# Cross attention and ternary feed-forward on one core: scores from two float32r row halves instead of six bfloat16 parts, and the copy of a group's sums on ScalarE

## The reference

```
q = rope(layernorm(x) @ Wq); k, v = split(ctx @ Wkv); k = rope(k)      # 32 heads of 16
w = softmax(q k^T / 4);  x = x + (w v) @ Wout + bout
u = absmax_quant(layernorm(layernorm(x)));  h = gelu(u @ ternary(w_fc)^T)
x = x + absmax_quant(layernorm(h)) @ ternary(w_proj)^T
```

## Time and profile before

| what | value |
|---|---|
| runs | 826.62, 828.09, 830.45 us |
| the profiled execution | 829.01 us; its span 826.9 us, 2.1 us lie around it |
| projection, to the first transposed score | 0 to 163 us |
| attention | 163 to 540 us |
| feed-forward | 540 to 827 us |
| TensorE / VectorE / ScalarE / GpSimd busy in the span | 782.2 / 683.7 / 454.8 / 337.3 us |

### The profile page before, as it was taken

The page is one execution under the profiler, slowest core; times in us unless marked ns, Lnnn a source line. Parts: engine busy times, 40 slices in busy tenths (PEclk is TensorE's granted clock), DMA queues, the critical chain, the costliest instruction groups (busy, mean ns, idle before and its releaser), DMA issues.

```text
span 826.9 us, 11697 instructions
## 1 busy us (share of the span) xinstructions
PE 782.2 (95%) x3842; PEld 333.4 (40%) x3842; DVE 683.7 (83%) x937; ACT 454.8 (55%) x825; POOL 337.3 (41%) x428
## 2 busy tenths in 40 slices
PE   1899999799999999999999999998999999999995
PEld 0788877122222222222232222243444444444442
DVE  5988876988888888888888887279999899899883
ACT  4477655177777777777777777642233322333230
POOL 3777866645434554455445554221113111111000
PEclk9999999599999999999999999999999999999998
DMA  8288886634555555665666663226565455643553
GB/s 280 83 213 237 251 232 169 160 102 124 142 142 143 153 147 137 155 141 162 167 157 166 170 167 74 72 76 104 115 130 126 90 112 111 121 101 77 102 114 90
DMA packets 175627, 116.14 MB, mean 140 GB/s; under 512 B 116560, under 2 KB 147280, under 8 KB 175568
## 3 DMA queue, kind: packets, MB, share of 16 engines
q1 hardware_dynamic: 175568, 115.40, 56.4%
HBM read 64.50 MB, written 25.43 MB: 109 GB/s over the span
## 4 chain that ended last, share of the span: by engine, by line
PE 72%; DVE 6%; ACT 1%; DMA 1%; issue 1%; POOL 1%; SPq 0%; DVEq 0%; POOLq 0%; ACTq 0%
PE banks L638 15%; PE banks L625 15%; PE banks L599 13%; PE banks L882 11%; PE banks L870 11%; PE banks L856 6%; DVE h_scales L948 1%; DVE maxima L669 1%; ACT probs_words L689 1%; DVE probs_words L957 1%; DVE h_stats L935 1%; PE banks L608 1%; DMA stack_words<-stack_words 1%; ACT probs_words L998 0%; DVE stack_words L963 0%
## 5 line engine op out<-in xcount | busy, mean ns | idle before, releaser
L669 DVE TENSOR_REDUCE maxima<-banks 128x2 f32<-128x1024 f32 x256 | 301.9, 1216 | 49.4 <-PE banks L599 49.4
L689 ACT ACTIVATE probs_words<-banks 128x512 f32<-128x512 f32 x512 | 275.8, 597 | 99.0 <-PE banks L625 97.3
L625 PE MATMUL banks<-stack_words 98*128 98x512 bf16 x512 | 174.9, 385 | 2.2 <-ACT probs_words L689 1.8
L599 PE MATMUL banks<-stack_words 96*128 96x512 bf16 x512 | 159.0, 392 | 4.9 <-DVE maxima L669 4.4
L638 PE MATMUL banks<-probs_words,late_words 128*32 128x512 f32 x1024 | 136.4, 605 | 0.5
L882 PE MATMUL banks<-ternary_words,stack_words 128*128 128x512 f16 x512 | 115.3, 384 | 5.4 <-DMA stack_words<-stack_words 5.4
L870 PE MATMUL banks<-ternary_words,late_words 128*128 128x512 f16 x512 | 114.8, 383 | 4.2 <-DMA late_words<-late_words 4.1
L998 ACT ACTIVATE probs_words<-probs_words,h_moments 128x2048 f32<-128x2048 f32 x16 | 32.0, 2002 | 126.5 <-DVE h_moments L940 126.5
L625 PEld LDWEIGHTS banks<-stack_words 98*128 98x128 bf16 x512 | 39.4, 97 | 142.3 <-ACT probs_words L689 85.1
L882 PEld LDWEIGHTS banks<-ternary_words,stack_words 128*128 128x128 f16 x512 | 50.5, 99 | 72.0 <-issue 16.2
L703 POOL TENSOR_SCALAR neg_max<-maxima 128x16 f32<-128x16 f32 x32 | 8.3, 259 | 172.0 <-DVE maxima L669 172.0
(11 more groups left out here) (123 smaller groups left out, 937.0 us busy)
## 6 DMA issues: line engine op xcount, KB each, us to landing
o_rows<-late_words SPq DMA_DIRECT2D x32, 256.0 KB, 2.6
k_parts<-ternary_words SPq DMA_DIRECT2D x48, 128.0 KB, 2.9
q_parts<-ternary_words SPq DMA_DIRECT2D x48, 128.0 KB, 2.5
stack_words<-q_parts SPq DMA_DIRECT2D x32, 192.0 KB, 2.9
stack_words<-k_parts SPq DMA_DIRECT2D x96, 64.0 KB, 2.7
stack_words<-k_parts SPq DMA_DIRECT2D x32, 192.0 KB, 2.7
attn_words<-in_x_dram SPq DMA_DIRECT2D x16, 256.0 KB, 4.4
probs_words<-in_L_ffn_w_fc_dram SPq DMA_DIRECT2D x16, 256.0 KB, 3.8
```

Of the source, the lines that this page charges most:

```text
L599: mm = self.nc.tensor.matmul(self.score_slot[j % 2][:, i], self.mem.q_stack[0:STACK, slot, head, c * P:(c + 1) * P], self.mem.k_stack[0:ST ...
L625: self.nc.tensor.matmul(self.mem.banks[:, self.ST_BANK[k]], self.mem.k_stack[0:STACK + 2, slot, head, c * P:(c + 1) * P], self.mem.q_stack ...
L669: dve.tensor_reduce(self.maxima[:, g % 2, 2 * j:2 * j + 2], self.score_slot[j % 2], AX.X, ALU.max).then_inc(self.scores_read, 1)
L689: act.activation(self.probs[:, c, head, :], self.mem.banks[:, self.ST_BANK[k]], ACT.Exp, scale=1 / math.sqrt(HEAD)).then_inc(self.exp_done, 1)
```

## The change

q and k are cut in two float32r parts instead of three bfloat16 parts. A stack has 48 rows for a head (three pairs of parts times 16), and two heads share the 128 partitions: one on rows 0 to 47, the other on rows 64 to 111 (with the maxima: to 49 and 113). Four heads are then two positions of two halves. A call of `scores` computes the same 128 queries for the two heads of a position, each half into a bank of its own; consecutive `scores_turned` alternate between the halves. In `tensor_step` the transposed score that stood right ahead of `weigh_v` moves ahead of the pair of row scores before it, so that transposed scores always come in pairs: two transposed, a pair of row scores, two transposed, a pair of row scores, `weigh_v`. `save_sums` goes from VectorE to ScalarE, behind the third exponential of the next group. `save_first` and `take_rest` replace `first_two`, `take_first` and `last_part`. `store_parts` issues eight DMAs of float32 instead of twelve of bfloat16, `load_stacks` eight instead of seven, and `load_max` two instead of one. `turn_max` runs in float32. Two memsets of the whole k stack give the ones by which the maxima are multiplied.

```diff
-PARTS = 3
-STACK = 6 * HEAD
+PARTS = 2
+HALF = 64
+STACK = 3 * HEAD
...
-        for s, part in ((0, 0), (0, 1), (1, 0), (0, 2), (1, 1), (1, 2)):
+        for s, part in ((0, 0), (0, 1), (1, 0), (1, 1)):
...
+    def take_rest(self, dve, n, s):
+        need(dve, self.parts_stored[n % 4 // 2], n // 4 * PAIR_STORES)
         dve.wait_ge(self.turned[s], n + 1)
         dve.wait_ge(self.first_done[s], n + 1)
+        dve.tensor_tensor(self.part_now(n, s, 1), self.turned_bank[s].rearrange("p (k c) -> p k c", k=KX),
+                          self.part_now(n, s, 0).bitcast(F32), ALU.subtract).then_inc(self.rest_done[s], 1)
...
+    def save_first(self, act, n, s):
         need(act, self.parts_stored[n % 4 // 2], n // 4 * PAIR_STORES)
         act.wait_ge(self.turned[s], n + 1)
         act.copy(self.part_now(n, s, 0), self.turned_bank[s].rearrange("p (k c) -> p k c", k=KX)
                  ).then_inc(self.first_done[s], 1)
-        act.wait_ge(self.rest_done[s], n + 1)
-        act.copy(self.part_now(n, s, 1), self.rest[s].rearrange("p (k c) -> p k c", k=KX)
-                 ).then_inc(self.second_done[s], 1)
...
-    def last_part(self, pool, n, s):
...
     def scores(self, pe, g, j):
+        pair, c, slot = j // CHUNKS, j % CHUNKS, g % STACK_SLOTS
...
+        for half in range(2):
+            rows = slice(half * HALF, half * HALF + STACK)
+            mm = self.nc.tensor.matmul(self.score_slot[j % 2][:, half],
+                                       self.mem.q_stack[rows, slot, pair, c * P:(c + 1) * P],
+                                       self.mem.k_stack[rows, slot, pair, :], start=True, stop=True)
...
     def scores_turned(self, pe, g, k):
+        pair, half = head // TWO, head % TWO
+        rows = slice(half * HALF, half * HALF + STACK + 2)
         self.nc.tensor.matmul(self.mem.banks[:, self.ST_BANK[k]],
+                              self.mem.k_stack[rows, slot, pair, c * P:(c + 1) * P],
+                              self.mem.q_stack[rows, slot, pair, :], start=True, stop=True
                               ).then_inc(self.st_ready, 1)
...
         for c in range(CHUNKS):
             if 0 <= turned < GROUPS:
                 self.scores_turned(pe, turned, 4 * c)
+                self.scores_turned(pe, turned, 4 * c + 1)
             if s < GROUPS:
                 self.scores(pe, s, 2 * c)
-            if 0 <= turned < GROUPS:
-                self.scores_turned(pe, turned, 4 * c + 1)
...
+    def save_sums(self, act, g):
+        need(act, self.o_stored[g % O_SLOTS], g // O_SLOTS * DMA)
+        act.wait_ge(self.pv_done, (g + 1) * CHUNKS)
+        act.copy(self.o_ring[:, g % O_SLOTS], self.pv_bank).then_inc(self.o_saved, 1)
...
                     if within(s - 2, GROUPS):
                         att.exponentials(act, s - 2, k)
+                    if k == 2 and within(s - 3, GROUPS):
+                        att.save_sums(act, s - 3)
```

More of the change, by code:

```diff
@@ L230, in store_parts @@
                 sp.dma_start(views[s][n // 4, g, part, :, :, pair * 2 * P:(pair + 1) * 2 * P],
-                             self.parts[g * GW:(g + 1) * GW, pair, s, part]).then_inc(self.parts_stored[pair], DMA)
+                             self.parts[g * GW:(g + 1) * GW, pair, s, part].bitcast(F32)
+                             ).then_inc(self.parts_stored[pair], DMA)
     def turn_inputs(self, pe, n):
@@ L286, in add_totals @@
         pe.wait_ge(self.ones_ready, 1)
-        self.nc.tensor.matmul(self.total_bank, self.ones[:], self.abs_sum[:], start=True, stop=True
+        self.nc.tensor.matmul(self.total_bank, self.ones, self.abs_sum[:], start=True, stop=True
                               ).then_inc(self.total_ready, 1)
@@ L520, in load_stacks @@
         for stack_sb, where, runs in (
-            (mem.q_stack, mem.q_parts, ((0, 0, 3), (3, 0, 2), (5, 0, 1))),
-            (mem.k_stack, mem.k_parts, ((0, 1, 1), (1, 0, 1), (2, 0, 1), (3, 0, 3))),
-        ):
-            src = where[g].rearrange("t (d h) c -> (t d) (h c)", h=GH)
-            for to, part, count in runs:
-                sp.dma_start(stack_sb[to * HEAD:(to + count) * HEAD, slot].rearrange("p h c -> p (h c)"),
-                             src[part * HEAD:(part + count) * HEAD]).then_inc(self.stacks_loaded[slot], DMA)
+            (mem.q_stack, mem.q_parts, ((0, 0, 2), (2 * HEAD, 1, 1))),
+            (mem.k_stack, mem.k_parts, ((0, 1, 1), (HEAD, 0, 2))),
+        ):
+            for half in range(2):
+                src = where[g].rearrange("t (d a j) c -> a t d (j c)", a=TWO, d=HEAD)[half]
+                for to, part, count in runs:
+                    rows = src[part]
+                    if count > 1:
+                        rows = rows.unsqueeze(0).to_broadcast([count, HEAD, GH // TWO * SEQ])
+                    first = half * HALF + to
+                    sp.dma_start(stack_sb[first:first + count * HEAD, slot].rearrange("p j c -> p (j c)").bitcast(F32), rows
+                                 ).then_inc(self.stacks_loaded[slot], DMA)
     def load_max(self, sp, g):
         sp.wait_ge(self.max_saved, g + 1)
-        sp.dma_start(self.mem.q_stack[STACK:STACK + 2, g % STACK_SLOTS].rearrange("p h (c q) -> p (h c) q", c=CHUNKS),
-                     self.max_rows[:, g % 2]).then_inc(self.max_loaded[g % STACK_SLOTS], DMA)
+        for half in range(2):
+            first = half * HALF + STACK
+            sp.dma_start(self.mem.q_stack[first:first + 2, g % STACK_SLOTS].bitcast(F32).rearrange("p j (c q) -> p (j c) q",
+                                                                                              c=CHUNKS),
+                         self.max_rows[half * GH * CHUNKS:(half + 1) * GH * CHUNKS, g % 2]
+                         ).then_inc(self.max_loaded[g % STACK_SLOTS], DMA)
     def load_weight(self, sp, w_fc, w_proj, n):
@@ L1173, in _ @@
                 for j in range(2 * GH):
-                    if j == 1 and s >= 3:
-                        att.save_sums(dve, s - 3)
                     if j == 4 and s >= 7 and s % 2 == 1:
```

135 lines of the change are left out of this document (51 added, 84 removed).

## The result

The changed kernel took 1023.4 us in the median of four runs (1002.67 to 1037.61); the kernel before took 828.12 on the same chip. The ratio is 1.216 (95% interval 1.209 to 1.223). The prediction was 840 us with a range of 819 to 860: the sign was right, the size wrong by more than ten times. The profiled execution took 1011.24 us with a span of 1009.4, against 829.01 and 826.9.

The account below looks back on a forecast made before the run. TensorE was taken to set the time, with a ScalarE loop nearly as long under it. From 829.0 us: +12.9 thirty steps, +1.7 two steps behind, +0.5 attention's start, -3.7 projection, 840.4, so 840 for a median; range 819 to 860.

Parts of the forecast that it names:

- the price of the stack loads: SyncE's queue in the projection: one more stack load was priced by its issue alone, 0.7 us.
- most of the 3.85 comes back: Projection's last tile: its x load leaves 1.9 to 2.2 us earlier, regaining 3.7 of 3.85 us lost on TensorE.
- In later steps the load has more than 1 us to spare: Attention after its start: the maxima row's load, now two, delays nothing; only the start pays, +0.5 us.
- DMAs are the limit: Lower bound of the projection's gain: 0 us instead of 3.7 if DMAs limit the last tile.
- the clock's chance of 0.04: Rival: TensorE, left idle by side-by-side pairs, drops to 1.2 GHz in the attention; +66 us, about 900; chance 0.04.
- Halves side by side: TensorE's scores: two half-height matmuls run in parallel, a pair costing 0.23 us, with 0.46 as bound.
- ordinary quarters: Attention, quarters from one `weigh_v` to the next without halfway wait or copy: 2.81 us against 2.84 before.
- halfway: The quarter with scores 8 and 9, where a transposed score needs the second exponential: 3.30 us against 3.09.
- ScalarE's own path of 2.66: Attention quarter: ScalarE's second exponential ends at 2.62 us, plus 0.04 to `weigh_v`, under TensorE's 2.81.
- the loads that don't show: Rival: float32r weight loads hide under `weigh_v` or waits, saving 0.10 us each; -0.27 a step, 819 us; chance 0.22.
- halves that take turns: Rival: half-height matmuls on TensorE run one after the other, 0.46 us a pair; +1.12 a step, 861; chance 0.16.
- a hidden copy: Rival: ScalarE's idle time takes the copy of the sums, without its 0.46 us; 830 us; chance 0.08.

Follow-up runs that it names:

- e8: The changed kernel with eight stack loads, none reading a row twice, and the parts stacked in another order: 867.62 us.
- e3: The kernel before the change, with q's repeated parts brought by repeating loads (six loads instead of seven, part pairs in another order): 900.23 us, ratio 1.086.
- e4: The changed kernel with twelve plain stack loads, row scores back between the transposed pairs and the copy of the sums back on VectorE: 852.16 us, ratio 1.031.
- e11: The changed kernel with eight loads without repeats and row scores back between the transposed pairs, the copy left on ScalarE: 832.65 us, ratio 1.002.
- e5: The changed kernel with twelve plain stack loads and each row score issued three times in groups 2 to 6: 862.77 us, ratio 1.038.
- e6: The changed kernel with twelve plain stack loads and two extra full-height matmuls ahead of the row scores in groups 2 to 6: 889.17 us, ratio 1.068.
- e7: The changed kernel with twelve plain loads, old order, copy on VectorE, and two extra full-height matmuls ahead of row scores in groups 2 to 6: 882.14 us.
- e12: The changed kernel with eight loads without repeats and the copy of the sums back on VectorE, the change's order kept: 858.88 us, ratio 1.027.
- e9: The changed kernel with eight loads without repeats, row scores back between the transposed pairs and the copy back on VectorE: 814.61 us, ratio 0.984.
- e1: The changed kernel with every stack load plain, twelve instead of eight: 869.94 us, ratio 1.037.

## Why the prediction was wrong

**The step that failed: the price of the stack loads.** "one more stack load costs (111.09 - 106.11) / 7 = 0.7", "most of the 3.85 comes back", "In later steps the load has more than 1 us to spare". All three count the time to issue a load and none the time to carry it out. The change replaces plain loads by repeating ones, and these occupy the DMA engines, as much as two of them can carry, for 10.7 us a step. The issue was forecast rightly (the last load of x left 2.3 us earlier, forecast 1.9 to 2.2), the landing was not, and everything behind them is late: the projection's last tile (16.38 between its transposes instead of the 7.07 forecast, so that 5.5 are lost where the bound "DMAs are the limit" stood at nothing gained), the first maxima row (16.03 of wait, where the kernel before had 0.2 and the forecast added 0.5) and 38.5 us of later waits (54.5 less 16.03). e8 shows that it is the repeats: with as many loads and bytes and none repeated, all of these go, and the load of x brings back 3.2 of the 3.85, near the 3.7 taken.

**The second: the clock's chance of 0.04.** Its mechanism was named, its size too low (a quarter of 3.9 and a step of 16 at 1.2 GHz, where 4.49 and 18.46 were measured), and it was set aside too lightly. Of the 163.4 us that the attention gained, 38.5 are later waits and 18.4 are e8's steps at full clock (390.0 us from first to last `weigh_v`, by its 410.1 less 20.1, against 371.6); the remaining 106.5 were not isolated by a run, and go with quarters of 4.49 and 4.98 at a granted clock of 0.50. Fifteen whole steps of the changed kernel last 18.28 to 18.46, much as the three slow ones of e8 (18.46), in which nothing is late; together they are some 94 us longer than fifteen steps of 12.17. A wait starts the fall, and the change's order prolongs it: the kernel before, made to wait by repeating loads, has its clock back after some 3 to 7 us (e3), and the halves in the old order, with VectorE's copy, after 3 to 10 (e4); in the changed kernel, behind its first waits, it is down for 7 to 68 us at a time. At the start of the attention the clock is at 0.50 for 78 us in the profiled execution of e8, and for 27 in that of e11, which differs by the order alone. Why the order does it is argued and not shown: that TensorE has less work in its waits fits e5's profile, but not the full-height matmuls of e6 and e7, and what exactly counts stays open.

**What held, where the clock was 1.00.** Halves side by side (0.23 a pair: the four extra pairs of a filled quarter, two of them in the wait, add 0.47). The first exponential 1.53 behind `weigh_v` (307.72 - 306.19), by the row of ScalarE:

```profile
307.72 2.06 ACT L682 ACTIVATE probs_words<-banks 128x512 f32<-128x512 f32 x4 [1.06 <-PE banks L624]
```

Also the ordinary quarters, 2.83 (2.81), halfway 3.33 (3.30), the copy's 3.16 (3.12), a step 12.16 (12.04). The copy's 0.31 over an ordinary quarter, which e12 measures as 0.29 a step. ScalarE's own path of 2.66, which became the quarter of e9, 2.67, once the order let it. The rivals of the loads that don't show, of halves that take turns and of a hidden copy are out by the same rows. The sum of these terms, 840, is near e8 without its slow clock, 842; that it is so near is partly luck, since e8's attention costs 3.8 us more than forecast (18.4 against 12.9 + 1.7) and its start 2.4 us less (5.6 us earlier against 3.7 - 0.5).

## What to carry to other kernels

Price a DMA by the engines that carry it, not only by its issue: look at the outermost dimension of both sides, and where a source repeats rows, arrange the copies so that they are contiguous or spend another load. Where a change makes matmuls cheaper and TensorE begins to wait, fill the wait with the work that is there (here the row scores, worth 0.58 a step and, by the medians of e8 with e12 and of e11, some 50 us of half clock) instead of putting it behind. And when an expected gain is missing, undo the parts one at a time: three of four parts of this change cost time, and the fourth, the halves with two parts, made the kernel 1.6% faster.

## What was not expected of the hardware

A repeating source of outer size 2 ran at 49 GB/s, and a load of 16 KB behind such ones was there 6.95 us after its issue. Full-height matmuls between half-height ones cost 0.33 us each instead of 0.23, and a kernel with them, put in to keep TensorE at work, had no less time at half clock (63 to 141 us in e6) than the one without (46 to 123 in e1). The profile can show TensorE busy for 30.00 of 30.00 us (185 to 215 in e1) while the granted clock stays at 0.50. Twelve loads of 0.46 us of issue each filled a queue that eight of them left free, and that was worth 38 us (852.16 against 814.61).
